# Attention products split into four 32-column matmuls, value products into two halves, and a new slot order on TensorE

## The reference, cut to what matters

```
q, k, v = proj(layernorm(x))                       # per batch and head: 2048 x 16
scores  = q @ k.T / sqrt(16)
decay   = sum_n softmax(mix)[h, n] * clip(dp[h, n]) ** |i - j|      # n = 0, 1
probs   = softmax(scores * decay)
x       = x + (probs @ v) @ Wo.T + bo
x       = x + relu(layernorm(x) @ Wq1.T + b1) @ Wq2.T + b2          # Wq1, Wq2 in {-1, 0, 1}
```

## Time and profile before

| | |
|---|---|
| median of the runs | 1789.03 us |
| the profiled execution | 1789.16 us, of which 1787.4 us span |
| TensorE busy | 1744.3 us, 98% |
| VectorE busy | 1558.8 us, 87% |
| ScalarE busy | 1345.2 us, 75% |
| attention, read as 131 to 1634 us | 1503.0 us |

### The profile page before, as it was taken

The page is one execution under the profiler, slowest core; times in us unless marked ns, Lnnn a source line. Parts: engine busy times, 40 slices in busy tenths (PEclk is TensorE's granted clock), DMA queues, the critical chain, the costliest instruction groups (busy, mean ns, idle before and its releaser), DMA issues.

```text
span 1787.4 us, 31962 instructions
## 1 busy us (share of the span) xinstructions
PE 1744.3 (98%) x11858; PEld 775.6 (43%) x11858; DVE 1558.8 (87%) x3664; ACT 1345.2 (75%) x1558; POOL 776.5 (43%) x405
## 2 busy tenths in 40 slices
PE   7979999999999999999999999999999999998998
PEld 4524444444444444444444444444444444444666
DVE  5879988999899989898999999898989999987885
ACT  5748687878787777878787878687878787667565
POOL 4009182726354554637271809181727364150110
PEclk9959999999999999999999999999999999999999
DMA  6884747474655546464637373747474645444541
GB/s 199 274 211 106 157 97 162 97 157 101 134 118 120 134 107 139 99 153 104 149 90 156 83 155 86 153 95 161 97 162 97 142 108 112 115 123 110 136 120 36
DMA packets 177835, 230.33 MB, mean 129 GB/s; under 512 B 92640, under 2 KB 113520, under 8 KB 167536
## 3 DMA queue, kind: packets, MB, share of 16 engines
q1 hardware_dynamic: 175744, 227.61, 54.6%
q0 software_dynamic: 80, 0.54, 0.2%
q10 hardware_dynamic: 1856, 0.14, 0.1%
HBM read 65.94 MB, written 36.45 MB: 57 GB/s over the span
## 4 chain that ended last, share of the span: by engine, by line
PE 87%; DVE 5%; ACT 1%; issue 1%; ACTq 0%; DVEq 0%
PE ring L1539 28%; PE ring L1492 27%; PE tile L1523 23%; PE tile L1520 3%; PE tile L1581 2%; PE ring L1600 2%; DVE part_max L1272 1%; PE ring L1506 1%; DVE qk L1362 1%; DVE z_lo L1358 1%; DVE stats L1334 1%; DVE decayed L1330 0%; ACT z_hi L1187 0%; PE ring L1567 0%; DVE lo L1314 0%
## 5 line engine op out<-in xcount | busy, mean ns | idle before, releaser
L1232 ACT ACTIVATE probs<-tile 128x1024 f32<-128x1024 f32 x1024 | 1000.3, 1023 | 331.4 <-PE tile L1520 183.8
L1272 DVE TENSOR_REDUCE part_max<-ring 128x1 f32<-128x512 f32 x1536 | 964.9, 683 | 122.1 <-PE ring L1492 120.1
L1492 PE MATMUL ring<-k_stack,q_stack 96*128 96x512 f16 (+2 forms) x3072 | 714.5, 314 | 11.2 <-SPq L211 9.7
L1523 PE MATMUL tile<-q_stack,k_stack 98*128 98x512 f16 (+2 forms) x2560 | 585.0, 326 | 0.3
L1539 PE MATMUL ring<-probs,v_ones 128*32 128x512 f32 x4096 | 546.8, 605 | 0.0
L1492 PEld LDWEIGHTS ring<-k_stack,q_stack 96*128 96x128 f16 x3072 | 263.9, 99 | 511.5 <-DVE part_max L1272 393.2
L1101 POOL TENSOR_TENSOR diag<-diag,row_max 128x1024 f32<-128x1024 f32 x64 | 121.6, 1900 | 629.9 <-DVE row_max L1285 629.9
L1523 PEld LDWEIGHTS tile<-q_stack,k_stack 98*128 98x128 f16 x2560 | 249.6, 98 | 275.0 <-ACT probs L1232 5.9
L188 POOL TENSOR_TENSOR decayed<-qk,table_in 128x1024 f32<-128x1024 f32 x120 | 282.9, 2363 | 8.0
L1274 DVE TENSOR_REDUCE part_max<-ring 128x1 f32<-128x384 f32 x512 | 279.6, 546 | 0.7 <-PE ring L1492 0.7
L202 POOL TENSOR_TENSOR lo<-decayed,hi 128x1024 f16<-128x1024 f32 x120 | 256.7, 2139 | 9.9 <-ACT hi L196 9.9
(11 more groups left out here) (154 smaller groups left out, 967.8 us busy)
## 6 DMA issues: line engine op xcount, KB each, us to landing
q_stack<-hi SPq DMA_DIRECT2D x320, 128.0 KB, 3.8
k_stack<-hi SPq DMA_DIRECT2D x128, 256.0 KB, 4.3
q_stack<-lo SPq DMA_DIRECT2D x160, 128.0 KB, 3.1
table_in<-table_scratch SPq DMA_DIRECT2D x64, 256.0 KB, 8.1
k_stack<-lo SPq DMA_DIRECT2D x64, 256.0 KB, 3.7
out_scratch<-heads_out SPq DMA_DIRECT2D x64, 256.0 KB, 3.3
k_stack<-hi SPq DMA_DIRECT2D x64, 128.0 KB, 3.4
lo<-out_scratch SPq DMA_DIRECT2D x32, 256.0 KB, 5.3
```

Of the source, the lines that this page charges most:

```text
L1232: nc.scalar.activation(probs[:, t % 4], tile[t % 2][:].rearrange("p a b -> p (a b)"), ACT.Exp, scale=1.0 / (SCALE * SCALE * HEAD_DIM ** 0. ...
L1272: nc.vector.tensor_reduce(out[:, k:k + 1], ring_bank(n), AX.X, ALU.max).then_inc(ring_free, 1)
L1492: last = nc.tensor.matmul(ring[:, n % RING, col:col + width], q_stack[h][0:STACK, q // UNIT_SLOTS, level, q0:q0 + P], k_stack[h][0:STACK, ...
L1523: last = nc.tensor.matmul(out, k_stack[h][:, level, kb * P:(kb + 1) * P], q_stack[h][:, half, level, col:col + width], start=bank not in s ...
```

## The change

Four things change, all in TensorE's program. No instruction of another engine changes.

- Each score matmul of 128 array columns becomes four, one on each group of 32 columns, which write 32 PSUM rows each and stream the same data.
- The float32 transposes of the raw blocks and of the maxima become plain float32 matmuls against the identity, in four and in two groups of 32 columns.
- Each value product is split in two halves of 256 columns (`AV_COLS`).
- The slot order becomes max 0, tile 0, max 1, tile 1, max 2, value half 0, max 3, value half 1.

```diff
-                        last = nc.tensor.matmul(ring[:, n % RING, col:col + width],
-                                                q_stack[h][0:STACK, q // UNIT_SLOTS, level, q0:q0 + P],
-                                                k_stack[h][0:STACK, level, first:first + width],
-                                                start=(j == 0), stop=True, skip_group_check=True)
+                        for r in range(0, P, QUARTER):
+                            last = nc.tensor.matmul(ring[r:r + QUARTER, n % RING, col:col + width],
+                                                    q_stack[h][0:STACK, q // UNIT_SLOTS, level, q0 + r:q0 + r + QUARTER],
+                                                    k_stack[h][0:STACK, level, first:first + width],
+                                                    start=(j == 0), stop=True, skip_group_check=True)
...
-                nc.tensor.transpose(ring[0:MAXROWS * LO_ROWS, n % RING, 0:P],
-                                    max_repeated[:].rearrange("p r b -> p (r b)"), ident[:]).then_inc(ring_full, 1)
+                for r in range(0, MAXROWS * LO_ROWS, QUARTER):
+                    last = nc.tensor.matmul(ring[r:r + QUARTER, n % RING, 0:P],
+                                            max_repeated[:].rearrange("p r b -> p (r b)")[:, r:r + QUARTER], ident[:],
+                                            start=True, stop=True, skip_group_check=True)
+                last.then_inc(ring_full, 1)
...
-                    if level == RAW:
-                        last = nc.tensor.matmul(out, diag[h][:, kb], ident[:], is_transpose=True,
-                                                start=bank not in started, stop=True, skip_group_check=True)
+                    for r in range(0, P, QUARTER):
+                        if level == RAW:
+                            last = nc.tensor.matmul(out[r:r + QUARTER], diag[h][:, kb, r:r + QUARTER], ident[:],
+                                                    start=bank not in started, stop=True, skip_group_check=True)
...
+                for part in parts:
+                    columns = slice(part * AV_COLS, (part + 1) * AV_COLS)
+                    for par in range(2):
+                        t = 2 * j + par
+                        for qt in range(2):
+                            row = (2 * par + qt) * ROWS
+                            first = qt * 512 + part * AV_COLS
+                            last = nc.tensor.matmul(acc[row:row + ROWS, columns], v_ones[h][:, t % BLOCKS],
+                                                    probs[:, t % 4, first:first + AV_COLS],
...
-                    if ahead:
-                        max_scores(s, s + LEAD, (0, 1), i, o)
...
+                    ahead_scores(0)
+                    tile_scores(0)
+                    ahead_scores(1)
+                    tile_scores(1)
                     if s == SLOTS - 1 and o == STEPS - 1:
...
+                        products(s - 1, o, (0, 1))
+                    ahead_scores(2)
+                    with_values(0)
+                    ahead_scores(3)
+                    with_values(1)
```

More of the change, by code:

```diff
@@ L47 @@
 MAXROWS = 2
+QUARTER = 32
+AV_COLS = 256
 SCALE = 32.0
@@ L1534, in products @@
                 for par in range(2):
[L1535 to L1545, removed]
+                    pe.wait_ge(exp_done, EXPS * o + 2 * j + par + 3)
+                for part in parts:
[7 more added lines that the diff above has]
+                                                    probs[:, t % 4, first:first + AV_COLS],
+                                                    start=(part == 0 and j % UNIT_SLOTS == 0),
+                                                    stop=(j % UNIT_SLOTS == UNIT_SLOTS - 1),
+                                                    skip_group_check=True)
+                            if part == 1 and j % UNIT_SLOTS == UNIT_SLOTS - 1 and (par, qt) == (0, 1):
+                                last.then_inc(probs_used, 1)
+                if 1 in parts:
+                    last.then_inc(acc_full if j % UNIT_SLOTS == UNIT_SLOTS - 1 else probs_used, 1)
             def attn_product(g):
@@ L1648, in step @@
-                    scores(2 * s + 1, o)
-                    if s == SLOTS - 1 and o == STEPS - 1:
[L1650 to L1661, removed]
+                    j = s if s == SLOTS - 1 and o == STEPS - 1 else s - 1
```

29 lines of the change are left out of this document (24 added, 5 removed).

## The result

The changed kernel takes 1833.7 us (median of 4 runs, 1830.8 to 1838.7) against 1788.8 of the kernel before on the same chip: 1.026 times as long, interval 1.023 to 1.028, so +45 us where +118 was forecast. It is slower, by less than half the forecast.

What follows compares the result with a forecast made beforehand. TensorE was taken as the bound, busy 98% of the span, with VectorE next. The terms -95 + 27 + 78 + 7 + 101 gave +118 us on 1789, rounded to 1908 us, range 1725 to 1990 us.

Steps and rivals of the forecast that it cites:

- rival C: TensorE in the attention runs out of instructions, at 55 ns per matmul and load: 2215 us in all; chance 0.11.
- term 7: Slot order and waits: VectorE gets its banks more evenly, ScalarE has room once slots are longer; worth nothing.
- term 5: Float16 waves (four matmuls side by side) of L1492 and L1523: 18 ns more each, 5632 times, +101 us.
- Terms 2 and 3: Value products in halves, 53 ns more per slot, +27 us; raw blocks as two-pass float32 matmuls, 0.152 us more, +78.
- Term 1: Each slot's two switches between 128 and 32 columns, 0.185 us together, go: -95 us.
- Term 4: Turn of the maxima: two passes of two matmuls, 0.240 us against 0.135, 64 times: +7 us.
- Term 6: Weight loads: four of 32 columns in place of one, run under the matmuls before; counted as nothing.
- Rival A: Waves: the 27 ns overhead belongs to float32's two passes, separate waves cost 3 ns; -58 us, 1731 us; chance 0.30.
- Rivals B and D: B: only float16 waves are free, 1806 us, chance 0.12. D: the 0.09 us belongs to type, switches stay, 2003 us, 0.04.

Runs made afterwards that it cites:

- experiment 6: Changed kernel with scores, tiles, turn and raw blocks in 128 columns again, value halves and new slot order kept: 1910.4 us, 1.068 of the kernel before.
- experiment 7: Changed kernel with value products whole (512 columns) after the third max item, all else 32 columns wide: 1798.4 us, 1.005 of the kernel before.
- experiment 8: Changed kernel with whole value products and the slot order from before the change, so the 32-column form alone: 1798.3 us, 1.005 of the kernel before.
- experiment 2: Changed kernel with ScalarE's casts cut to 1/16 of the elements, the rest left uncast: 1806.8 us, 1.010 of the kernel before.
- experiment 1: Changed kernel with loads of q, k and tables bringing 128 of 2048 columns, the rest left out: 1767.5 us, 0.988 of the kernel before.

## Why the prediction was partly right

Slower was right, but by luck. The reason given, dearer waves, isn't there. By its matmuls alone the changed kernel is faster (1740.7 us with both other causes taken out), and it became slower by two costs that the prediction put at nothing: instructions that come late (66 us; no term has them, and rival C looked only at the engine's pace) and ScalarE (27 us, term 7). The steps that failed are therefore term 5, 101 us too high, and these two zeros, together 93 us too low. Terms 2 and 3 were too high by another 65 or so. By its own steps:

- **Term 1, the switches (-95): gone, as forecast.** Slots show no 0.09 us at the values, and experiment 6, which doubles the switches, costs the expected sum of switches and waves. The division of this sum between terms 1 and 2 is not shown.
- **Term 5, float16 waves (+101): the step that failed.** I put 18 ns on each wave because "the shape is the same" as the float32 wave. Measured is 0.217 us per wave, as for one matmul of 128 columns (0.216). The 27 ns were read from the distance behind a first pass that followed a switch; passes in succession show 6 ns (experiment 7). A price read next to a switch was applied to a stream without switches. The lower end, about 0, holds.
- **Terms 2 and 3 (+27, +78): mis-sized by the same 27 ns.** Value halves take 0.44 us for two passes, 0.87 for four, against 0.907 before: near their lower end, -22. Raw blocks are near theirs, +54: a slot with two of them is 0.35 us longer than one without (2.96, 2.61), where it was 0.13, which makes 0.11 us more for each.
- **Term 4 (+7)** is too small to tell. **Term 6 (0)** is right for the weight loads as work of the engine: they hid; a slot with raw blocks holds 24 score, 24 tile, 16 raw and 16 value matmuls, 80 with their loads, in 2.96 us without a gap, 37 ns for each. **The slot order** of term 7 is nothing (experiment 8).
- **Term 7, ScalarE "has room once slots are longer": wrong,** because they became shorter. It costs 27 us (experiment 2).
- **Rival A** has the size of the waves right and the reason wrong. It put the 27 ns down to float32's two passes, and in experiment 7 these cost 6 ns. Its 1731 us is close to the 1740.7 measured with both other causes taken out. Of the 9 us between, three stalls at record 193 in the attention (4.3 us) can hold a part; the rest stays open. And A gave no other cost.
- **Rivals B and D** are out: float32 waves are as cheap as float16 ones (0.22 us for a pass of 256 columns), and no gap stands where the types meet.
- **Rival C** asked whether TensorE runs out of instructions and answered by the engine's own pace. That pace was no limit (37 ns against its 55). The supply was: 66 us from late blocks, with the time at the lower clock behind some of the long stalls.

The sum of what was measured: 1740.7 + 66 + 27 = 1833.7, the result. Of what the prediction wanted to see, VectorE's idle time in the attention is 160 us (1546 less 1386), not 270. One sign it named for being wrong did appear, long idle times of TensorE with ScalarE as releaser.

Shown by the runs is that the stalls shrink when the loads shrink (60.4 to 7.4 us) or move (to 27.5), and that they do not exist in the kernel before or in experiment 6, with 94 and 130 blocks of 256 records. That TensorE waits for a packet is read from the records: the same place of every block, and at all 31 stalls a packet that ended 1.2 to 1.7 us before. No experiment changed the queue itself. What triggers the fetch of a block, and why it was not asked for earlier, stays open.

The split of the 66 us can be estimated from experiment 1. With fewer loads the stalls shrink from 60.4 to 7.4 us, and 25 distances of 0.2 us that remain without a stall make that 48 us of standing still. The 31 us at half clock are worth 15. Together that is 63 of the 66.

## What to carry to other kernels

Read the price of an instruction from a place where the new kernel's conditions hold: a wave beside a drain cost 27 ns above its stream, and waves in succession 3 to 6. A change that makes three times as many instructions makes the instruction stream a customer of the DMA engines, so look at what else these carry, and move a large load before giving the change up. When the bound engine speeds up, compare the next engine with it slot by slot, waits included, and not by its average: ScalarE at 75% still cost 27 us.

## What the runs showed of the hardware

- TensorE can stand still for up to 3.2 us in the midst of a product, with all operands there, at the same place of every 16 KB of its instructions, behind full DMA engines. It went on 1.2 to 1.7 us after a packet of instructions had ended.
- Behind a stall of 3.17 us the granted clock fell to its 1.2 GHz level (0.43 us for a wave of 0.217), for 3.4 us. It fell behind 8 of the 31 stalls at record 193, and not behind others with 2.4 and 2.5 us of idle time. Over the span the mean fell from 0.987 to 0.977 in the profiled execution. The busy share does not show this, since slow matmuls count as work.
- The four column groups do not keep step with each other. The records of one group of a later product can stand before another group's of the product ahead; in the changed kernel 9, then 1, then 3 matmuls of two lines alternate:

```profile
922.46 0.38 PE L1551 MATMUL ring<-probs,v_ones 128*32 128x256 f32 x1
922.47 0.23 PE L1495 MATMUL ring<-k_stack,q_stack 96*32 96x128 f16 x3
922.52 0.61 PE L1551 MATMUL ring<-probs,v_ones 128*32 128x256 f32 x7
```
- Waiting for loads to land before issuing more can be far worse than the crowding: a small urgent transfer behind them came up to 14.2 us late.
